# Splitting the attention's final sums into chunks on GpSimd, and the first spreading inside the attention's body

## The reference

```python
deg = jnp.clip(adj.sum(axis=1), 1.0)
dis = deg ** (-0.5)
diffusion = (dis[:, None] * adj * dis[None, :]) @ x - x
sim = x @ x.T / (norms[:, None] * norms[None, :])
attn = jax.nn.softmax(beta * sim * adj, axis=1)
x1 = layernorm(x + diffusion + sigmoid(alpha) * (attn @ x - x))
# layer 1
XW = x1 @ W
den = exp(leaky_relu(s_row[:, None] + s_col[None, :]))
num = A @ den
att = where(num != 0, den / num, 0)
out = layernorm(x1 + A @ (att @ XW))
```

## Time and profile before

| | |
|---|---|
| three runs | 666.08, 668.66, 668.97 us; median 668.66 |
| the profiled execution | 667.4 us, span 665.6 us |
| mean granted TensorE clock | 0.944 |
| TensorE busy | 573.8 us, 86% of the span |
| VectorE busy | 527.7 us, 79% |
| GpSimd busy | 424.3 us, 64% |
| ScalarE busy | 369.8 us, 56% |

### The profile page before, as it was taken

One profiled execution on the slowest core, in us unless ns is written; L12 is line 12 of the kernel. 1 busy time (PEld: TensorE's weight loads), 2 busy tenths in 40 slices (PEclk: granted clock), 3 DMA queues, 4 the chain that ended last, 5 costly groups with the idle time before them and its releaser, 6 DMA issues.

```text
span 665.6 us, 11419 instructions
## 1 busy us (share of the span) xinstructions
PE 573.8 (86%) x4169; PEld 353.2 (53%) x4169; DVE 527.7 (79%) x965; ACT 369.8 (56%) x613; POOL 424.3 (64%) x447
## 2 busy tenths in 40 slices
PE   0899999999886879999727988898989999979993
PEld 0455545554332668888627644344445444447883
DVE  3889999889999073678878776899899999985442
ACT  3654444444765342579994426787777788851000
POOL 6799999999896033555414043778685788403663
PEclk9999999999998689999856999999999999988998
DMA  7999993000000000000000041233333333100100
GB/s 128 107 108 107 104 334 127 1 2 0 1 1 2 4 1 17 18 17 18 17 9 17 9 126 47 54 88 96 88 91 89 92 93 84 43 3 15 29 29 16
DMA packets 19924, 37.20 MB, mean 56 GB/s; under 512 B 2586, under 2 KB 11054, under 8 KB 19854
## 3 DMA queue, kind: packets, MB, share of 16 engines
q0 software_dynamic: 7392, 24.32, 20.5%
q1 hardware_dynamic: 12462, 11.98, 5.6%
HBM read 48.72 MB, written 10.45 MB: 89 GB/s over the span
## 4 chain that ended last, share of the span: by engine, by line
PE 44%; DVE 26%; POOL 12%; issue 9%; ACT 6%; DMA 1%; SPq 1%; DVEq 0%; POOLq 0%; ACTq 0%
POOL R L427 10%; PE PSALL L1919 8%; PE PSALL L1621 6%; PE PSALL L1818 5%; DVE ring L1410 4%; DVE ring L1403 4%; PE PSALL L1544 3%; PE PSALL L1747 3%; ACT AW L696 3%; PE PSALL L1878 3%; PE PSALL L1600 3%; DVE ring L998 3%; DVE AW L1003 2%; DVE FR L1410 2%; DVE FR L1403 1%
## 5 line engine op out<-in xcount | busy, mean ns | idle before, releaser
L427 POOL TENSOR_TENSOR R<-R,ring 128x452 f32<-128x452 f32 x120 | 164.2, 1406 | 2.4 <-ACT ring L618 2.4
L618 ACT ACTIVATE ring<-ring,sm 128x452 f32<-128x452 f32 (+1 forms) x132 | 86.5, 669 | 92.2 <-DVE ring L998 91.8
L1544 PE MATMUL PSALL<-XN 128*128 128x452 f16 (+2 forms) x396 | 97.9, 357 | 5.5 <-DVE ring L998 5.3
L1003 DVE TENSOR_TENSOR AW<-ring 128x452 bf16<-128x452 f32 x84 | 94.4, 1124 | 0.0
L1818 PE MATMUL PSALL<-AW,R 128*128 128x452 fp8e4 (+1 forms) x348 | 77.5, 354 | 16.6 <-DVE R L1342 10.3
L998 DVE TENSOR_TENSOR ring<-PSALL,AT 128x452 f32<-128x452 f32 (+1 forms) x132 | 79.5, 616 | 7.0 <-PE PSALL L1544 6.3
L488 POOL DMA_INDIRECT AW<-ATd,FR x44 | 55.2, 1255 | 32.4 <-DVE FR L1293 17.7
L1878 PE MATMUL PSALL<-ring,XW 128*128 128x452 bf16 (+1 forms) x300 | 67.7, 360 | 1.0 <-DVE ring L1410 1.0
L1544 PEld LDWEIGHTS PSALL<-XN 128*128 128x128 f16 (+1 forms) x396 | 37.0, 97 | 58.2 <-issue 20.1
L1621 PE MATMUL PSALL<-R,AT 128*128 128x256 f16 x484 | 62.2, 289 | 2.5 <-issue 2.5
L1410 DVE TENSOR_TENSOR ring<-ring 128x904 bf16<-128x904 f32 (+1 forms) x50 | 62.5, 1251 | 0.0
(11 more groups left out here) (284 smaller groups left out, 1088.8 us busy)
## 6 DMA issues: line engine op xcount, KB each, us to landing
AT<-in_adjT POOLq DMA_DIRECT2D x22, 338.5 KB, 35.1
ATd<-AT SPq DMA_DIRECT2D x2, 3723.5 KB, 18.5
X<-in_x SPq DMA_DIRECT2D x2, 704.0 KB, 6.0
XWd<-ring SPq DMA_DIRECT2D x11, 128.0 KB, 1.8
out<-ring SPq DMA_DIRECT2D x21, 64.0 KB, 1.5
AW<-ATd,FR POOLq DMA_INDIRECT x44, 4.3
X<-XWd,idx POOLq DMA_INDIRECT x22, 2.5
Wt<-in_W SPq DMA_DIRECT2D x1, 64.0 KB, 3.4
```

The source lines that it names most:

```text
L427: i = G.tensor_tensor(ES_, ES_, z, ALU.add)
L618: S.activation(z, z, ACT.Exp, scale=bcol[0:rows, :]).then_inc(s_exp, 1)
L1003: V.tensor_tensor(low_of(q)[0:rows, :], ring[0:rows, q % 6, 0:w], upper(q, rows, w), ALU.subtract).then_inc(s_low, 1)
L1544: m = TE.matmul(PSALL[0:rows, b, 0:w], lh[:, jt * P:jt * P + rows], rh[:, c0:c0 + w], start=(k == 0), stop=(k == 2))
```

## The change

GpSimd's copy and its subtraction are each cut into six, one for each chunk of columns; all six copies come first. `s_es` now ends at 12, and TensorE's row sums wait for 12. `spread(0)` is called as the last thing in the attention's body, in both bodies, ahead of the branch; the first round of the loop that follows no longer calls it. The function stands higher in the file and waits for the parts of `AT` itself, which inside the attention's body have been met already. The waits for the 22 parts of `AT` and for the weights ahead of the loop stay.

```diff
             gp.wait_ge(s_esum, NE)
-            G.tensor_copy(ESh, ES[:, 0:N]).then_inc(s_es, 1)
-            gp.wait_ge(s_es, 1)
-            G.tensor_tensor(ESl, ES[:, 0:N], ESh, ALU.subtract).then_inc(s_es, 1)
+            for c0, w in CH:
+                G.tensor_copy(ESh[:, c0:c0 + w], ES[:, c0:c0 + w]).then_inc(s_es, 1)
+            for c, (c0, w) in enumerate(CH):
+                gp.wait_ge(s_es, c + 1)
+                G.tensor_tensor(ESl[:, c0:c0 + w], ES[:, c0:c0 + w], ESh[:, c0:c0 + w], ALU.subtract).then_inc(s_es, 1)
...
                         m.then_inc(s_gather, 1)
+                spread(0)
+
+            def spread(it):
+                if it < 4:
+                    pe.wait_ge(s_aotA, it + 1)
+                for t in range(T):
+                    pe.wait_ge(s_AT[t], 16)
+                for k, (t0, nt) in enumerate(SL):
+                    pe.wait_ge(s_xp, k + 1)
...
-                pe.wait_ge(s_es, 2)
+                pe.wait_ge(s_es, 2 * NC)
...
             for it in range(T):
                 if it >= 4:
                     pe.wait_ge(s_tail, TAIL * (it - 4) + 2)
-                spread(it)
+                if it:
+                    spread(it)
```

More of the change, by code:

```diff
@@ L1602, in attention @@
                         m.then_inc(s_gather, 1)
+                spread(0)
[6 more added lines that the diff above has]
+                    pe.wait_ge(s_xp, k + 1)
+                    for jt in range(t0, t0 + nt):
+                        ins = TE.matmul(PSALL[:, it % 4, 0:2 * D], AT[:, jt, it * P:(it + 1) * P], xp[:, jt, :, :].rearrange("p c d -> p (c d)"),
+                                        start=(jt == 0), stop=(jt == T - 1))
+                ins.then_inc(s_spread, 1)
             pe.wait_ge(s_flag, 1)
@@ L1612, in _ @@
             pe.only(met)
[L1615 to L1623, removed]
             def xw_part(part, g):
```

## The result

| | before | after |
|---|---|---|
| median of 7 runs each, us | 668.66 (666.08 to 670.05) | 665.09 (662.92 to 665.75) |
| ratio after/before, 95% | | 0.9949 [0.9927, 0.9972] |
| profiled execution, us (span) | 667.4 (665.6) | 663.7 (661.9) |

The changed kernel is 3.6 us faster, 0.51%; 6.1 were forecast. 665.09 is inside the range (659.0 to 666.3), at the upper end of the forecast's own (660.3 to 665.2). The two profiled executions differ by 3.7 us, so one can look in them for where the rest went.

What follows compares the result with a forecast made beforehand. No single bound: at the attention's end GpSimd's long instructions hold VectorE, then branch delay and spreading follow. 2.8 + 3.7 - 0.4 = 6.1 us gained, median 662.6 us; own range 660.3 to 665.2, 8 in 10 659.0 to 666.3.

Steps and rivals of the forecast that it cites:

- What bounds: Attention's end: VectorE's L1003 waits while GpSimd's long cast or subtraction runs; 6.3 us of waiting to be removed.
- Part 1: Attention's end: GpSimd's twelve short steps let VectorE in sooner; 2.8 us gained, range 1.8 to 4.2.
- part 2: First spreading moved ahead of the branch, its matmuls covering the branch's delay; 3.7 us gained, range 2 to 5.
- The sequencer's bound: Behind the attention's branch: TensorE's sequencer is through branch and waits at 213.2 + 0.8 + 5.1 = 219.1, when transposes begin.
- 22 more cost it 0.7 to 0.8 us: Ahead of the branch: handing over the spreading's 22 matmuls costs TensorE's sequencer 0.7 to 0.8 us, at 31 ns each.
- One sign of the prediction: Behind the first spreading: transposes begin within 0.5 us of its end if the clock is at half.
- Rival 2: Attention's branch: queued matmuls do not cover it, 2.5 us stand behind the spreading; 665.1 us, chance 0.16.
- Rival 1: Attention's end: TensorE's clock stays up, later spreadings gain 3.6 us together; 658.6 us, chance 0.10.
- Rival 3: Attention's tail: GpSimd's next step always gets in ahead of a waiting L1003; 666.0 us, chance 0.08.
- Rival 4: `spread(1)` to `spread(6)`: clock stays at 1.2 GHz, 9.7 us more against 6.5 gained; 671.9 us, chance 0.04.
- nothing there waits for a transfer begun before the attention's end, so 6.5 us pass through, but for the clock: After the row sums, to the kernel's end: the whole 6.5 us gain passes through, but for the clock.
- I set 0.4 for that: `spread(1)`: may take 4.75 us instead of 3.85, VectorE's third division up to 0.9 late; 0.4 us deducted.

Runs made afterwards that it cites:

- late_sub: After, with GpSimd's six subtractions held back until VectorE has done its last L1005; 663.02 us, 0.9917 of before.
- calm kernels: `fill3_before`, `fill3_steps` and `fill3_after`: unused matmuls in three places where TensorE waits, to hold the clock up; 663.49, 661.08 and 658.36 us.
- after_again: After, unchanged, timed and profiled a second time; 664.32 us, 0.9953 of before.
- no_waits: After without the 22 waits for parts of `AT` ahead of the transposes; 663.28 us, 0.9935 of before.
- spread_only: Before with the first spreading moved ahead of the branch, GpSimd's two long instructions kept; 668.83 us, 1.0014 of before.
- fill: After with 14 unused matmuls ahead of layer 1's loop, where TensorE waited 3.00 us for a DMA; 661.29 us, 0.9898 of before.
- fill_before: Before with 14 unused matmuls ahead of layer 1's loop; 669.91 us, 1.0036 of before.
- combo_fill: After with subtractions held back, 22 waits left out, nine unused matmuls and part of layer 1's work ahead of its loop; 660.76 us, 0.9898 of before.
- fill3_after: After with unused matmuls: 14 at layer 1's start, 11 at its end, 7 ahead of the output's matmuls; 658.36 us, 0.9857 of before.
- fill3_before: Before with unused matmuls: 14 at layer 1's start, 11 at its end, 7 ahead of the output's matmuls; 663.49 us, 0.9932 of before.
- fill3_steps: Before with GpSimd's twelve short steps alone and 14, 11 and 7 unused matmuls in three places; 661.08 us, 0.9890 of before.

## Why the prediction was right, and where it was short

**What bounds: right.** GpSimd's long instructions held VectorE, and with them gone the attention ends earlier. The last L1005 ends at 209.0 + 3.7 = 212.7 us; 213.2 was worked out. The row sums begin at 220.7 (220.1), and GpSimd's steps end at 208.01 + 7.55 = 215.6 (216.3), 5 us ahead of the row sums that need them. The last three L1005 cost 1.23 us each (3.69 for the three), where 1.5 were worked out and the earlier trace rows has 1.03 in the median, and `late_sub` shows the cost by taking it away (1.68 for the three).

**Part 1 and part 2: the sum right, the split too near to call.** In the calm kernels the transposes begin at 225.77, with the steps alone at 222.05 and with both at 219.26: 3.7 us for the steps and 2.8 for the moved spreading, where 2.8 and 3.7 were forecast. The last low half ended at 216.17, 213.19 and 212.51, so the steps moved VectorE by 3.0 (forecast 2.8), and the remainder came on TensorE. Counted from GpSimd's first copy, whose start differs between the three (203.11, 202.53, 202.76), it is 3.1 and 3.0. In the kernels without fillings, part 2's 3.7 us never reached the median: the steps alone gained as much (0.995) as the whole change (0.9949 and 0.9953). In single profiled executions such tenths move: `after_again` has its last L1005 2.1 us later than after, at 214.78, after a clock of 0.83 from 163 to 173 us and again from 195 to 205. The window of the second, first in after, then in `after_again`:

```profile
195.00:205.00 10.00, 8.04 (x33) 2.46 (x31) 10.00 (x13) 5.34 (x10) 9.61 (x8) 1.00 0.02 4
```

```profile
195.00:205.00 10.00, 8.03 (x27) 2.29 (x26) 8.27 (x12) 4.31 (x8) 9.62 (x8) 0.83 0.01 2
```

**The sequencer's bound: right in kind, 1.1 us short.** The mis-sized term is "22 more cost it 0.7 to 0.8 us". The transposes should begin 0.8 + 5.1 = 5.9 us after the last L1005. They came 7.05 us after it (219.72 - 212.67), the last 0.89 of it "issue" behind a spreading at half clock; 6.2 in `late_sub`; and 5.9 in `no_waits`, where the spreading at half clock was the bound. The traces show where the 1.1 us lie. The packet of instructions starts 1.0 us after the last L1003 in before and 3.1 us after the last L1005 in after: 22 matmuls ahead of the branch delay it by 2.1 us (the same in five kernels), not by 0.8. It starts 1.8 us after the spreading's first matmul in eight profiles, so the sequencer reaches the branch only when a part of the 22 has been worked off. One sign of the prediction missed with it: the transposes were to come within 0.5 us of a spreading at half clock, and came 0.89 us behind it. That VectorE ended 0.5 us earlier than worked out hid about half of the error.

**Rival 2 (the branch isn't covered): refuted for the change as it is, true in part.** It wanted 2.5 us behind the spreading; after has 0.89. It is there as 2.05 in `spread_only` and 2.78 in `late_sub`, so the branch's delay stays in the sequencer and queued matmuls hide it for as long as they last. The page "Runtime: NRT & Kernel Launch", section "Instruction fetch mechanics", of the Trainium skill says that a taken branch out of the loaded pages forces a fetch before execution goes on; the prediction drew from it that the delay stays wherever the branch stands. The traces agree that a delay stays (0.89 to 2.78 us of it in sight in after, `spread_only` and `late_sub`) and add that queued matmuls hide a part of it. The measured 665.09 us is also rival 2's own number (665.1), by coincidence: in the profile of after 0.89 us of its 2.5 are there, and the rest of the shortfall is elsewhere.

**Rival 1 (the clock stays up): not in after.** It was 0.50 from 214.0 to 218.9. `late_sub` keeps it up there, and the sequencer takes the gain back. **Rival 3: refuted** by the longest L1005 of the tail, 1.46 us. **Rival 4 (slower): refuted**, since `spread(2)` and `spread(3)` took 2.56 us again and the shift had grown to 6.4 us at layer 1.

**The step that fell short** is "nothing there waits for a transfer begun before the attention's end, so 6.5 us pass through, but for the clock", with "I set 0.4 for that". The mechanism was named, its size wasn't: the text priced the clock only at `spread(1)` and stopped there. At `spread(1)` itself the price was near: it took 4.86 us instead of 3.85, and the third division came 5.2 us earlier where the transposes had come 5.9, so 0.7 late; by layer 1 that was made up. What happened behind it, in the profiled execution: 1.7 us at layer 1's start, by a fall of the clock that `fill` took away again, and 1.2 us in the output (matmuls from first to last 55.9 us against 54.7), together about 2.9, less what the shift had gained by then (6.4 against 6.1). In medians: 3.6 us where 6.1 were forecast, and 5.1 when the clock is held up at those places in both kernels. That last figure still misses 1.0 us, which is within its interval. That the measured time is inside the forecast's own range, by 0.1 us, owes something to the range's width. The ends given for the two parts make it 659.9 to 665.3 and not 660.3 to 665.2, and a subtraction of 452 columns scaled from 0.91 us for 384 is 1.07, not 1.04; `late_sub` has 1.0 (six in 6.03). Neither changes a reading.

**What stays open.** The falls of the clock were seen in profiled executions alone, one or two of a kernel; each run has its mean clock on record, but not where it fell, so what the falls take from the 3.6 us can't be given exactly. Why the clock falls at layer 1's start with the moved spreading, and not without it, isn't settled; before and after wait 3.0 us for the same DMA there. The moved spreading with the fillings but without the steps was not run.

## What to carry to other kernels

Cut a long GpSimd instruction into short ones where VectorE has to get in beside it: here that alone gained as much as the whole change. Matmuls handed over ahead of a branch do hide a part of its delay, but here that gain showed in the time only once the clock was held up behind it. A gain made in the middle of a kernel must be followed to its end, landmark by landmark: of 6.4 us, 2.7 were lost behind it, to the clock and to a stall at a branch. Filling the waits of TensorE with matmuls nobody needs was worth more than the change (5.1 us, 663.5 against 668.6, where the change had 3.6). But in the kernel before the first group alone made it slower; of the other groups none was tried alone.

## What the runs showed of the hardware that was not expected

**A second stall behind a branch, which moves with the code.** The output's 22 transposes come behind layer 1's branch. They were one piece in before, and had a gap of 0.97 us after 15, of 1.53 after 9 and of 2.39 after 2 in after, `fill_before` and `combo_fill`. The 14 matmuls of `fill_before`, each with a weight load, put 28 more instructions ahead of that place, and the gap appeared behind the ninth. In the three kernels that differ from after only on GpSimd or not at all ahead of that place (`after_again`, `late_sub`, `spread_only`) it stays after 15. In all six kernels with the gap a packet of 16 KiB on the queue of instructions lands 1.2 to 1.4 us before the matmuls go on (in after at 590.16 us, and they go on at 591.37). That it is code being loaded is argued from these times; no run changed the loading alone. The page "Runtime: NRT & Kernel Launch", section "Instruction fetch mechanics", of the Trainium skill has blocks of 16 KiB that are fetched one ahead and calls the cost of crossing one mostly hidden; if this is such a crossing, it isn't hidden here, close behind a branch. With 11 matmuls queued ahead of the branch the transposes are one piece again, in `fill3_after` behind 0.27 us of "issue". Whether those matmuls hid the gap or only moved it out of the 22 isn't shown.

**Redundant waits have a price.** Twenty-two waits, all met long before, cost TensorE's sequencer about 1.2 us behind the branch (2.7 to 2.9 us from the packet's landing to the next matmul with them, 1.5 without). In the medians it can't be told from nothing (0.9935 against 0.9953).

**The clock's falls differ between executions of one kernel.** From layer 1's first group to its fourth, after took 20.50 us and `after_again` 21.97; it was 18.82 in `fill`, `fill3_before`, `fill3_steps` and `fill3_after`. The first fall, at layer 1's start, is in both executions; `after_again` has a second one, at the third group (2.98 us instead of 1.70).
